# A two-layer graph network on one core: paired angles, a sum moved between passes, and indirect DMAs alternating one by one

## The chip, the cores and the metric

The kernel runs on one core of a Trainium2 chip. The metric is the time of one execution on the device, in microseconds (us). TensorE is called PE, its weight load PEld, VectorE DVE, ScalarE ACT, GpSimd POOL, and SyncE SP (SPq for its queue). SP does nothing but issue plain DMAs; POOL issues the indirect ones, which gather or scatter 128 rows by a list of indices.

## The reference, cut to what matters

There are 100,000 nodes with 160 features (64 scalars and 32 vectors of 3) and 25,000 edges, sorted by destination. Each layer norms the rows, takes relu, sends a message along each edge, sums the messages by destination, and adds the result to x.

```
h = relu(layernorm(x))
# layer 0
sc    = linear(h, sc_w)                      # every node
msg   = f(linear(h[src], lin1_w), edge_attr, silu(edge_scalars @ fc_w1) @ fc_w2)
mid   = segment_sum(msg, dst) / 4
conv  = linear(mid, lin2_w)
angle = 0.1 * (mid_s @ lin3_w) / sqrt(96) * node_attr
x1 = x + cos(angle) * sc * node_attr + sin(angle) * conv * node_attr
# layer 1
h1  = relu(layernorm(x1))
m   = g(h1[src], edge_attr; W1..W5)
agg = segment_sum(m, dst)
out = x1 + h1 + relu(linear(agg, Ws, Wv))
```

## The kernel before, in words

The work is done in three passes over DRAM. **Pass one** takes all nodes as if none had a message (dense part: x1, h1 and out = x1 + h1) and beside it computes the messages of layer 0 for 196 tiles of 128 edges (T = 196), sums them by destination, and stores the sums (`sum_tab`) and the own rows of the destinations (`own_tab`). It ends at about 1205 us. **Pass two** mends the nodes that have messages: for each of 49 groups (Q = 49) of four tiles it loads own rows and sums, makes x1 and h1, scatters h1 into `h1_all` and stores x1 + h1 in `y_tab`. **Pass three** gathers h1 of the sources, computes the messages of layer 1, sums them, adds y, and scatters the result into `out`.

The order of the work is written out by hand, engine by engine; semaphores tie the engines. Each engine's instructions run in the order in which they stand, so a wait holds up all that is behind it on its engine. `At(i, c)` is the number of a step in a loop; `q.times(m, plus)` is q*m + plus, `q.over(k, m, plus)` is (q // k)*m + plus, and `q.mod(k)` picks a buffer.

Pass two runs in steps. In step q **DVE** does (`p2_step`, L1647): the moments of group q, the first part of the scales of q-1 (L1592; it waits for the sines of q-1), the centring of q (L1553, L1554), the angles of q in eight short instructions (`p2_angle`, L1564 to L1581) strewn between the others, the sum x1 + h1 of group q-3 (`p2_y`, L1645), the rest of the scales of q-1, the self part of q-1 (L1610), the second norm of q-2 (L1636, L1235), x1 of q-1 (L1620) and its moments. **PE** transposes the centred rows of q and multiplies them; **ACT** does in step q (L938): the roots, the copies of q's transposed rows (L918, L919), h1 of q-2 (L911), the sines of q (L924). Sine and root need different tables, each loaded by an ACT_TABLE_LOAD. **SP** (L545) loads in its step v the own rows of v when x1(v-4) is done, then the sums of v-1, and then stores y(v-6). DVE's step q makes x1(q-1), so that SP's step v falls into DVE's step v-3. **POOL** scatters h1 of each group, four DMAs (L727).

Pass three has one slot per tile. In slot n DVE takes the vector products of tile n (`p3_features`, L1719), the outer part of message n-2 (L1739, which waits for PE), the dot and cross products of n (L1730 to L1732), the output of tile n-4 (`p3_out`, L1755: the instruction called yo below), the message sum of n-2 (L1745), and once in four slots the selectors (L1406). PE transposes the features of n-1, sums n-4 and multiplies n-2. ACT scales and copies. POOL (L746 to L774) issues two scatters of `out` (tiles n-4 and n-3), then two gathers of h1 rows (tiles n+6 and n+7), and so on. The four gathers of a group count up one semaphore, `m_g[j]`; DVE and ACT wait for all four (64) at the first tile of the group. The first instruction behind DVE's wait is a copy of indices (L1409). `y_tab` is loaded once a group into x1 (`p3_y`, L576).

Of the kernel before, what the change touches and what calls it, by code (L numbers as in the profile page):

```python
# [73 lines left out]
def gnn_kernel(nc, xa, src, dst, dst_rows, number, edges_in, scalars_in, scalars_t_in, wpack, out):  # L74
# [19 lines left out]
    y_tab = scratch("y_tab", (Q, P, GQ * D))  # L94
# [24 lines left out]
    with ExitStack() as ctx:  # L119
# [96 lines left out]
        trig = [two(f"trig{n}", [P, 2 * GQ]) for n in range(8)]  # L216
# [112 lines left out]
        r_y = sem("p2_y_ready")  # L329
        r_put = sem2("p2_h1_scattered")  # L330
        r_sty = sem2("p2_y_stored")
# [6 lines left out]
        m_y = sem2("p3_y_loaded")  # L338
        m_g = sem2("p3_h1_rows")
# [36 lines left out]
        def _(sp):  # L376
# [181 lines left out]
            for v in range(Q - 1, Q + 6):  # L558
                p2_step(At(0, v))
# [32 lines left out]
            for j in range(2):  # L592
                sp.wait_ge(r_sty[j], 16 * ((Q + 1 - j) // 2))
                sp.wait_ge(r_put[j], 64 * ((Q + 1 - j) // 2))
# [11 lines left out]
        def _(pool):  # L606
# [136 lines left out]
            pool.wait_ge(r_y, Q)  # L743


            def p3_gather(n):  # L746
# [3 lines left out]
                wait(pool, m_ft, n.times(1, -6))  # L750
                wait(pool, m_ss, n.times(1, -6))
                gather(h1_all, h1[j], D, i_src[j], m_g[j], (t, t + 1))

            def p3_scatter(n):
# [3 lines left out]
                pool.wait_ge(m_o, n.times(1, 2))  # L758
                scatter(out, yo[j], i_put[j], m_put[j], (t, t + 1))

            for n in range(0, 6, 2):
                p3_gather(At(0, n, 8))
            for n in range(0, 8, 2):
                if n >= 4:
                    p3_scatter(At(0, n - 4, 8))
                p3_gather(At(0, n + 6, 8))
            with pool.Fori(1, (Q - 3) // 2) as i:
                for c in range(0, 8, 2):
                    p3_scatter(At(i, c, 8) - 4)
                    p3_gather(At(i, c, 8) + 6)  # L770
            for n in range(T - 3 * GQ, T + 4, 2):
                p3_scatter(At(0, n - 4, 8))
                if n + 6 < T:
                    p3_gather(At(0, n + 6, 8))  # L774
# [3 lines left out]
        def _(act):  # L778
# [142 lines left out]
            def p2_sines(q):  # L921
                j = q.mod(2)
                act.wait_ge(r_ang, q.times(8, 8))
# [14 lines left out]
            def p2_step(q):  # L938
# [7 lines left out]
                if q.within(Q):  # L946
# [278 lines left out]
        def _(v):  # L1225
# [331 lines left out]
            def p2_angle(q, part):  # L1557

                j = q.mod(2)
                ang, turns, rest, arg = (trig[n][j] for n in range(4))  # L1560
                k = turns[:, GQ:2 * GQ]
                if part == 0:
                    v.wait_ge(r_cv[q.mod(4)], q.over(4, 16, 16))
                    ins = V.tensor_tensor(ang[:, 0:GQ], x3(cv[q.mod(4)], CW, GQ)[:, :, 0], x3(x_q[q.mod(4)], XW, GQ)[:, :, D],  # L1564
                                          ALU.mult)
                else:
                    v.wait_ge(r_ang, q.times(8, part))
                if part == 1:
                    ins = V.tensor_scalar(turns[:, 0:GQ], ang[:, 0:GQ], 1.0 / PI2, ROUND, ALU.mult, ALU.add)
                elif part == 2:  # L1570
                    ins = V.tensor_scalar(turns[:, GQ:2 * GQ], turns[:, 0:GQ], -ROUND, None, ALU.add)
                elif part == 3:
                    ins = V.scalar_tensor_tensor(rest[:, 0:GQ], k, -CA, ang[:, 0:GQ], ALU.mult, ALU.add)
                elif part == 4:
                    ins = V.scalar_tensor_tensor(rest[:, GQ:2 * GQ], k, -CB, rest[:, 0:GQ], ALU.mult, ALU.add)
                elif part == 5:
                    ins = V.scalar_tensor_tensor(ang[:, GQ:2 * GQ], k, -CC, rest[:, GQ:2 * GQ], ALU.mult, ALU.add)
                elif part == 6:
                    ins = V.tensor_scalar(arg[:, 0:GQ], ang[:, GQ:2 * GQ], PI_IN, -PI_IN, ALU.min, ALU.max)
                elif part == 7:  # L1580
                    ins = V.tensor_scalar(arg[:, GQ:2 * GQ], arg[:, 0:GQ], 0.5, None, ALU.mult)  # L1581
# [287 lines left out]
```

## Time and profile before

| | us |
|---|---|
| three runs | 2253.13, 2264.83, 2266.06 |
| their median | 2264.83 |
| the profiled execution, its time | 2256.09 |
| its span | 2254.3 |
| PE busy | 1753.3 (78%) |
| DVE busy | 1726.3 (77%) |
| POOL busy | 1517.9 (67%) |
| ACT busy | 1441.7 (64%) |

The span is the time from the first to the last instruction that the profiler saw. The busy shares are means over three passes of different kinds; what holds for one pass has to be read in a window of that pass. All durations below come from the one profiled execution. A busy time counts an instruction from its start to its end, and instructions of one engine overlap a little, so that the distance of two starts says more than a duration.

### The profile page before, as it was taken

What the parts mean: (1) busy time and instruction counts of PE and PEld (TensorE: products, weight loads), DVE (VectorE), ACT (ScalarE), POOL (GpSimd) and SP (SyncE); (2) the same over time, 40 slices, a digit from 0 to 9 for tenths busy, and PEclk for the clock granted to TensorE, in tenths of its full rate; (3) what the DMA queues carried; (4) which work ended last, traced back from release to release, by engine and by line L of the source; (5) the groups of instructions that cost most, each with busy time, mean ns of one, the idle gap of its engine ahead of it and who ended that gap; (6) DMA issues with size and microseconds to landing.
All of it is one profiled execution on the core that took longest, in us unless ns stands there. A gap on an engine that the chain in (4) does not pass through costs nothing.

```text
span 2254.3 us, 52147 instructions
## 1 busy us (share of the span) xinstructions
PE 1753.3 (78%) x12130; PEld 1645.3 (73%) x12130; DVE 1726.3 (77%) x6714; ACT 1441.7 (64%) x4193; POOL 1517.9 (67%) x1636
## 2 busy tenths in 40 slices
PE   6898988898998989898995666666467767677665
PEld 2798988888888989888885665565366666666665
DVE  2699899989999998999896999999455555555553
ACT  2588887788787878877886777777333333333332
POOL 3378888888878788878873555555566666666664
PEclk9999999999999999999996556666599999989998
DMA  5477677767777777767775445554333333333331
GB/s 188 144 245 248 246 247 243 246 245 250 248 254 247 250 250 244 245 243 245 244 243 189 151 157 170 168 161 162 93 88 86 96 94 96 97 90 95 100 94 58
DMA packets 176960, 408.91 MB, mean 181 GB/s; under 512 B 43774, under 2 KB 73788, under 8 KB 176766
## 3 DMA queue, kind: packets, MB, share of 16 engines
q1 hardware_dynamic: 129694, 333.90, 43.0%
q0 software_dynamic: 47232, 74.64, 11.8%
q8 instruction: 11, 0.18, 0.0%
q14 instruction: 23, 0.19, 0.0%
HBM read 199.20 MB, written 216.96 MB: 185 GB/s over the span
## 4 chain that ended last, share of the span: by engine, by line
PE 35%; DVE 25%; issue 15%; ACT 10%; DMA 8%; POOL 4%; DVEq 1%; SPq 1%; ACTq 0%; POOLq 0%
DVE st L1231 6%; DMA h<-h_all,i_src 5%; PE bank L1007 5%; ACT h L786 3%; PE bank L1002 3%; DVE st_e L1231 3%; PE bank L1008 3%; PE bank L1111 3%; PE bank L1183 2%; PE bank L1085 2%; DMA h_all<-h,i_put 2%; PE bank L1056 2%; DVE part L1610 2%; POOL h L622 2%; DVE x L1379 2%
## 5 line engine op out<-in xcount | busy, mean ns | idle before, releaser
L678 POOL TENSOR_TENSOR yo<-x,h 128x320 f32<-128x320 f32 x392 | 363.1, 947 | 122.6 <-ACT h L786 115.3
L1007 PE MATMUL bank<-wp,hT 128*128 128x160 f32 x1568 | 374.2, 320 | 0.0
L786 ACT ACTIVATE h<-x,nmr,inv 128x160 f32<-128x160 f32 x784 | 342.0, 514 | 0.6 <-DVE nmr L1235 0.6
L629 POOL DMA_INDIRECT h_all<-h,i_put x196 | 206.1, 1051 | 190.5 <-issue 163.2
L629 POOL DMA_INDIRECT out<-yo,i_put x196 | 200.1, 1021 | 187.7 <-DVE yo L1755 119.5
L1007 PE MATMUL bank<-wp,eT 128*128 128x160 f32 x784 | 262.6, 428 | 49.4 <-ACT eR L919 43.6
L1008 PE MATMUL bank<-wp,hR 128*128 128x64 f32 x1568 | 259.4, 247 | 0.0
L1183 PE MATMUL bank<-ident,feat 128*128 128x128 f32 x392 | 90.4, 314 | 213.7 <-DVE feat L1732 187.7
L1008 PEld LDWEIGHTS bank<-wp,hR 128*128 128x128 f32 x1568 | 255.5, 190 | 0.0
L1379 DVE SCALAR_TENSOR_TENSOR x<-bank,scl,x_all 128x160 f32<-128x160 f32 x784 | 253.8, 365 | 1.0 <-PE bank L1008 0.6
L622 POOL DMA_INDIRECT x_e<-in_xa,i_src x200 | 211.5, 1057 | 44.5 <-issue 18.0
L622 POOL DMA_INDIRECT h<-h_all,i_src x196 | 196.9, 1005 | 62.8 <-issue 57.3
L1007 PEld LDWEIGHTS bank<-wp,hT 128*128 128x128 f32 x1568 | 237.8, 192 | 0.0
L622 POOL DMA_INDIRECT x_d<-in_xa,i_dst x196 | 197.2, 1006 | 59.0 <-issue 58.3
L1739 DVE TENSOR_TENSOR xr<-bank,q_ed 128x96 f32<-128x96 f32 x196 | 50.3, 256 | 237.0 <-PE bank L1193 237.0
L1183 PEld LDWEIGHTS bank<-ident,feat 128*128 128x128 f32 x392 | 41.1, 146 | 246.9 <-DVE feat L1732 156.8
L1231 DVE BATCH_NORM_STATS2 st<-x 128x6 f32<-128x320 f32 x490 | 218.3, 486 | 0.0
L971 ACT ACTIVATE tot<-bank 128x160 f32<-128x160 f32 x196 | 59.0, 301 | 248.5 <-PE bank L1205 247.7
L1007 PEld LDWEIGHTS bank<-wp,eT 128*128 128x128 f32 x784 | 163.0, 258 | 65.7 <-issue 34.9
L965 ACT ACTIVATE feat<-h,q_ed 128x160 f32<-128x160 f32 x196 | 83.5, 426 | 162.7 <-DMA h<-h_all,i_src 157.9
L1111 PE MATMUL bank<-ident,feat 128*128 128x128 f32 x588 | 101.4, 282 | 109.0 <-DVE feat L1453 61.8
L1008 PEld LDWEIGHTS bank<-wp,eR 128*128 128x128 f32 x784 | 180.4, 261 | 0.0
(164 smaller groups left out, 5556.7 us busy)
## 6 DMA issues: line engine op xcount, KB each, us to landing
x_all<-in_xa SPq DMA_DIRECT2D x98, 644.0 KB, 5.7
h_all<-h SPq DMA_DIRECT2D x98, 640.0 KB, 3.7
out<-yo SPq DMA_DIRECT2D x98, 640.0 KB, 4.0
q_row<-row_tab SPq DMA_DIRECT2D x98, 256.0 KB, 3.6
sum_tab<-tot SPq DMA_DIRECT2D x49, 322.0 KB, 3.7
own_tab<-x_d SPq DMA_DIRECT2D x49, 322.0 KB
x_all<-own_tab SPq DMA_DIRECT2D x49, 322.0 KB, 2.9
y_tab<-yo SPq DMA_DIRECT2D x49, 320.0 KB
```

The lines of the kernel that those rows point to most:

```text
L622: nc.gpsimd.indirect_dma_start(into[:, t * width:(t + 1) * width], None, rows, bass.IndirectOffsetOnAxis(ap=index[:, t:t + 1], axis=0)).th ...
L629: nc.gpsimd.indirect_dma_start(rows, bass.IndirectOffsetOnAxis(ap=index[:, t:t + 1], axis=0), tiles_of[:, t * D:(t + 1) * D], None, bounds ...
L678: ins = nc.gpsimd.tensor_tensor(yo[j][:, a:b], x1[j][:, a:b], h1[j][:, a:b], ALU.add)
L786: ins = nc.scalar.activation(h1[j][:, k * D:(k + 1) * D], x1[j][:, k * D:(k + 1) * D], ACT.Relu, bias=nmr2[j][:, k:k + 1], scale=inv2[j][: ...
L965: nc.scalar.activation(f[:, 0:D], h, ACT.Copy, scale=ed(j, t, 0, 1))
L1002: nc.tensor.transpose(ps_main[:, t * P:(t + 1) * P], main[:, t * P:(t + 1) * P], ident[:, :])
L1007: nc.tensor.matmul(dst_ps, main[:, t * P:(t + 1) * P], wp[:, w:w + D], start=True, stop=False)
L1008: return nc.tensor.matmul(dst_ps[:, 0:DS], rest[:, :], wp[:, w + D + t * DS:w + D + (t + 1) * DS], start=False, stop=True)
L1111: ins = nc.tensor.transpose(bank[4][:, c * P:(c + 1) * P], f[:, at:at + P], ident[:, :])
L1183: nc.tensor.transpose(b[:, c * P:(c + 1) * P], f[:, c * P:(c + 1) * P], ident[:, :])
L1231: return V.bn_stats(st[:, 2 * pair:2 * pair + 2, :].rearrange("p g k -> p (g k)"), two_rows[:, 0:D, :])
L1379: ins = V.scalar_tensor_tensor(x1[j][:, k * D:(k + 1) * D], bank[2 + pair % 2][:, k % 2 * D:(k % 2 + 1) * D], scl1[u.mod(4)][:, k:k + 1], ...
```

## The change

It has three parts. **Angles.** `p2_angle` runs in even steps alone and takes groups q and q+1 together; its first part waits for own rows and sums of both. The sines and the halved sine's square are taken once for two groups as well. **The sum** x1 + h1 leaves pass two: SP stores x1 and h1 of each group in two tables, pass three loads both, and DVE adds them there once per four tiles (`p3_x1_h1`). On SP the store now stands first in a step, for group v-5. **Pass three's DMAs:** POOL alternates one scatter (tile n-4) and one gather (tile n+5); each tile's gather has a semaphore of its own, and DVE and ACT wait for it tile by tile. The copy of the gather's indices moves from the first to the last tile of a group.

```diff
             def p2_store(q):
-                sp.wait_ge(r_y, q.times(1, 1))
-                sp.dma_start(y_tab[q.times(1)], yo[q.mod(2)][:, 0:GQ * D]).then_inc(r_sty[q.mod(2)], 16)
+                j = q.mod(2)
+                sp.wait_ge(r_x1, q.times(2, 2))
+                sp.dma_start(x1_tab[q.times(1)], x1[j][:, 0:GQ * D]).then_inc(r_stx[j], 16)
+                sp.wait_ge(r_h1, q.times(1, 1))
+                sp.dma_start(h1_tab[q.times(1)], h1[j][:, 0:GQ * D]).then_inc(r_sth[j], 16)
 
 
             def p2_step(v):
+                if (v - 5).within(Q):
+                    p2_store(v - 5)
                 if v.within(Q):
                     p2_own(v)
                 if (v - 1).within(Q):
                     p2_sums(v - 1)
-                if (v - 6).within(Q):
-                    p2_store(v - 6)
 
             for v in range(8):
                 p2_step(At(0, v))
             with sp.Fori(2, Q // 4) as i:
                 for c in range(4):
                     p2_step(At(i, c))
-            for v in range(Q - 1, Q + 6):
+            for v in range(Q - 1, Q + 5):
                 p2_step(At(0, v))
...
             def p3_y(q):
                 j = q.mod(2)
                 wait(sp, m_o, q.times(GQ, -GQ))
-                sp.dma_start(x1[j][:, 0:GQ * D], y_tab[q.times(1)]).then_inc(m_y[j], 16)
+                sp.dma_start(x1[j][:, 0:GQ * D], x1_tab[q.times(1)]).then_inc(m_y[j], 16)
+                sp.dma_start(hb[j][:, 0:GQ * D], h1_tab[q.times(1)]).then_inc(m_y[j], 16)
 
...
             p2_scatter(At(0, Q - 1))
             for j in range(2):
                 pool.wait_ge(r_put[j], 64 * ((Q + 1 - j) // 2))
-            pool.wait_ge(r_y, Q)
+                pool.wait_ge(r_sth[j], 16 * ((Q + 1 - j) // 2))
 
 
             def p3_gather(n):
                 j, t = n.c // GQ % 2, n.mod(4)
                 if t == 0:
                     pool.wait_ge(m_ix, n.over(4, 1, 1))
-                wait(pool, m_ft, n.times(1, -6))
-                wait(pool, m_ss, n.times(1, -6))
-                gather(h1_all, h1[j], D, i_src[j], m_g[j], (t, t + 1))
+                wait(pool, m_ft, n.times(1, -7))
+                wait(pool, m_ss, n.times(1, -7))
+                gather(h1_all, h1[j], D, i_src[j], m_g[n.mod(8)], (t,))
 
             def p3_scatter(n):
                 j, t = n.c // GQ % 2, n.mod(4)
                 if t == 0:
                     pool.wait_ge(m_px, n.over(4, 1, 1))
-                pool.wait_ge(m_o, n.times(1, 2))
-                scatter(out, yo[j], i_put[j], m_put[j], (t, t + 1))
-
-            for n in range(0, 6, 2):
+                pool.wait_ge(m_o, n.times(1, 1))
+                scatter(out, yo[j], i_put[j], m_put[j], (t,))
+
+            for n in range(5):
                 p3_gather(At(0, n, 8))
-            for n in range(0, 8, 2):
-                if n >= 4:
-                    p3_scatter(At(0, n - 4, 8))
-                p3_gather(At(0, n + 6, 8))
+            for n in range(8):
+                if n >= GQ:
+                    p3_scatter(At(0, n - GQ, 8))
+                p3_gather(At(0, n + 5, 8))
...
             def p2_h1(q):
                 j = q.mod(2)
                 act.wait_ge(r_nmr, q.times(2, 2))
-                wait(act, r_y, q.times(1, -1))
+                wait(act, r_sth[j], q.over(2, 16))
                 wait(act, r_put[j], q.over(2, 64))
...
             def p2_sines(q):
-                j = q.mod(2)
-                act.wait_ge(r_ang, q.times(8, 8))
+                j = q.mod(4) // 2
+                act.wait_ge(r_ang, q.over(2, 8, 8))
                 nc.scalar.activation(trig[4][j][:, :], trig[3][j][:, :], ACT.Sin).then_inc(r_sin, 1)
...
             def p3_scalars(n):
                 j, t = n.c // GQ % 2, n.mod(4)
                 if t == 0:
-                    act.wait_ge(m_g[j], n.over(8, 64, 64))
                     act.wait_ge(m_tb[j], n.over(8, 16, 16))
+                act.wait_ge(m_g[n.mod(8)], n.over(8, 16, 16))
...
             def p2_angle(q, part):
 
-                j = q.mod(2)
-                ang, turns, rest, arg = (trig[n][j] for n in range(4))
-                k = turns[:, GQ:2 * GQ]
+                ang, turns, rest, arg = (trig[n][q.mod(4) // 2] for n in range(4))
+                k = turns[:, GP:2 * GP]
                 if part == 0:
-                    v.wait_ge(r_cv[q.mod(4)], q.over(4, 16, 16))
-                    ins = V.tensor_tensor(ang[:, 0:GQ], x3(cv[q.mod(4)], CW, GQ)[:, :, 0], x3(x_q[q.mod(4)], XW, GQ)[:, :, D],
-                                          ALU.mult)
+                    for d in range(2):
+                        if (q + d).within(Q):
+                            m = (q + d).mod(4)
+                            v.wait_ge(r_g[m], (q + d).over(4, 16, 16))
+                            v.wait_ge(r_cv[m], (q + d).over(4, 16, 16))
+                            ins = V.tensor_tensor(ang[:, d * GQ:(d + 1) * GQ], x3(cv[m], CW, GQ)[:, :, 0],
...
 
                 j = q.mod(2)
-                sines, half2, scales = trig[4][j], trig[5][j], trig[6][j]
+                sines, half2, scales = (trig[n][q.mod(4) // 2] for n in (4, 5, 6))
+                a, b = j * GQ, (j + 1) * GQ
                 attr = x3(x_q[q.mod(4)], XW, GQ)[:, :, D]
                 if part == 0:
                     v.wait_ge(r_sq1, q.times(1, 1))
-                    v.wait_ge(r_sin, q.times(1, 1))
+                    v.wait_ge(r_sin, q.over(2, 1, 1))
                     V.reciprocal(inv_e[j][:, :], sd_e[j][:, :])
-                    V.tensor_tensor(scales[:, GQ:2 * GQ], sines[:, 0:GQ], attr, ALU.mult)
-                    ins = V.tensor_tensor(half2[:, 0:GQ], sines[:, GQ:2 * GQ], sines[:, GQ:2 * GQ], ALU.mult)
+                    ins = V.tensor_tensor(scales[:, GP + a:GP + b], sines[:, a:b], attr, ALU.mult)
+                    if j == 0:
+                        ins = V.tensor_tensor(half2[:, 0:GP], sines[:, GP:2 * GP], sines[:, GP:2 * GP], ALU.mult)
                 elif part == 1:
                     v.wait_ge(r_scl, q.times(4, 1))
-                    V.tensor_tensor(scl_e[j][:, :], inv_e[j][:, :], attr, ALU.mult)
-                    ins = V.tensor_scalar(half2[:, GQ:2 * GQ], half2[:, 0:GQ], -2.0, 1.0, ALU.mult, ALU.add)
+                    ins = V.tensor_tensor(scl_e[j][:, :], inv_e[j][:, :], attr, ALU.mult)
+                    if j == 0:
+                        ins = V.tensor_scalar(half2[:, GP:2 * GP], half2[:, 0:GP], -2.0, 1.0, ALU.mult, ALU.add)
                 else:
                     v.wait_ge(r_scl, q.times(4, 2))
...
             def p2_x1(q):
                 j = q.mod(2)
                 v.wait_ge(r_scl, q.times(4, 4))
-                wait(v, r_y, q.times(1, -1))
+                wait(v, r_h1, q.times(1, -1))
+                wait(v, r_stx[j], q.over(2, 16))
                 for t in range(GQ):
...
-            def p2_y(q):
-                j = q.mod(2)
-                v.wait_ge(r_h1, q.times(1, 1))
-                wait(v, r_sty[j], q.over(2, 16))
-                V.tensor_tensor(yo[j][:, 0:GQ * D], x1[j][:, 0:GQ * D], h1[j][:, 0:GQ * D], ALU.add).then_inc(r_y, 1)
-
...
                 if a:
                     p2_centre(q)
+                if e:
                     p2_angle(q, 0)
-                if (q - 3).within(Q):
-                    p2_y(q - 3)
-                if a:
+                if e:
                     p2_angle(q, 1)
                 if b:
                     p2_scales(q - 1, 1)
-                if a:
+                if e:
                     p2_angle(q, 2)
                 if b:
                     p2_scales(q - 1, 2)
-                if a:
+                if e:
                     p2_angle(q, 3)
                 if b:
                     p2_self(q - 1)
-                if a:
...
             def p3_features(n):
                 j, t = n.c // 4 % 2, n.mod(4)
                 if t == 0:
-                    v.wait_ge(m_g[j], n.over(8, 64, 64))
                     v.wait_ge(m_tb[j], n.over(8, 16, 16))
-                    if (n + 8).within(T):
-                        index_copy(i_src[j], t_src, At(n.i, n.c // GQ, 2) + 2, m_ix)
+                v.wait_ge(m_g[n.mod(8)], n.over(8, 16, 16))
+                if t == GQ - 1 and (n + 5).within(T):
...
+            def p3_x1_h1(n):
+                j = n.c // GQ % 2
+                v.wait_ge(m_y[j], n.over(8, 32, 32))
+                V.tensor_tensor(x1[j][:, 0:GQ * D], x1[j][:, 0:GQ * D], hb[j][:, 0:GQ * D], ALU.add).then_inc(m_ys, 1)
+
             def p3_out(n):
                 j, t = n.c // GQ % 2, n.mod(4)
                 if t == 0:
-                    v.wait_ge(m_y[j], n.over(8, 16, 16))
+                    v.wait_ge(m_ys, n.over(4, 1, 1))
                     wait(v, m_put[j], n.over(8, 64))
                     index_copy(i_put[j], t_put, At(n.i, n.c // GQ, 2), m_px)
...
                     p3_message_sum(n - 2)
+                if n.mod(4) == 2 and (n - 2).within(T):
+                    p3_x1_h1(n - 2)
```

The rest of the diff carries the same names through (semaphores, tables, the columns of `trig`, the loops' ends) and makes the other parts of `p2_angle` twice as wide.

## Rows read from the trace of the kernel before

**Rows 1.** Windows of passes two, three: busy us per engine, PEclk, DMA share, GB/s.

```profile
1195.00:1590.00 395.00, 249.77 (x1036) 225.02 (x1034) 356.51 (x1573) 287.55 (x550) 205.86 (x198) 0.60 0.50 163
...
1613.00:2242.00 629.00, 441.06 (x2925) 405.10 (x2924) 331.36 (x1505) 233.11 (x967) 384.62 (x380) 0.93 0.32 90
```

**Rows 2.** Pass two's timeline, DVE, ACT, SP: start us, us, instruction, [idle before, releaser].

```profile
1492.04 0.18 DVE L1592 RECIPROCAL inv_e<-sd_e 128x4 f32<-128x4 f32 x1 [0.40 <-ACT trig L924]
...
1493.17 0.82 DVE L1645 TENSOR_TENSOR yo<-x,h 128x640 f32<-128x640 f32 x1
1493.91 0.16 DVE L1569 TENSOR_SCALAR trig<-trig 128x4 f32<-128x4 f32 x1
...
1496.01 0.16 DVE L1235 SCALAR_TENSOR_TENSOR nmr<-st,inv 128x4 f32<-128x4 f32 x1
1496.22 1.27 DVE L1620 SCALAR_TENSOR_TENSOR x<-cv,trig,part 128x160 f32<-128x160 f32 x4
...
1499.82 0.18 DVE L1592 RECIPROCAL inv_e<-sd_e 128x4 f32<-128x4 f32 x1 [0.46 <-ACT trig L924]
...
1522.78 0.18 DVE L1592 RECIPROCAL inv_e<-sd_e 128x4 f32<-128x4 f32 x1 [0.40 <-ACT trig L924]
...
1495.10 0.27 ACT L919 ACTIVATE eR<-bank 128x128 f32<-128x128 f32 x1
1496.34 1.76 ACT L911 ACTIVATE h<-x,nmr,inv 128x160 f32<-128x160 f32 x4 [0.97 <-DVE nmr L1235]
...
1497.66 0.34 SPq L534 DMA_DIRECT2D x_all<-own_tab  x1
1498.31 0.33 SPq L538 DMA_DIRECT2D hb<-sum_tab  x1
```

**Rows 3.** DMA issues of pass two: size, median us from issue to landing.

```profile
x_all<-own_tab SPq DMA_DIRECT2D x21, 322.0 KB, 2.9
...
cv<-sum_tab SPq DMA_DIRECT2D x11, 322.0 KB, 3.8
```

**Rows 4.** Timeline of pass two's start, SP and DVE: the first sums.

```profile
1209.59 0.43 SPq L538 DMA_DIRECT2D cv<-sum_tab  x1
...
1215.30 0.17 DVE L1564 TENSOR_TENSOR trig<-cv,x_all 128x4 f32<-128x4 f32 x1 [1.86 <-DMA cv<-sum_tab]
```

**Rows 5.** Timeline of pass three over one group's border, DVE, then POOL.

```profile
1907.61 0.31 DVE L1755 SCALAR_TENSOR_TENSOR yo<-tot,x 128x160 f32<-128x160 f32 x1
...
1909.85 0.26 DVE L1739 TENSOR_TENSOR xr<-bank,q_ed 128x96 f32<-128x96 f32 x1 [1.32 <-PE bank L1193]
...
1912.69 0.26 DVE L1739 TENSOR_TENSOR xr<-bank,q_ed 128x96 f32<-128x96 f32 x1 [1.32 <-PE bank L1193]
...
1916.17 0.17 DVE L1409 COPY i_src<-t_src 128x4 int32 x1 [1.75 <-DMA h<-h_all,i_src]
...
1916.61 0.25 DVE L1739 TENSOR_TENSOR xr<-bank,q_ed 128x96 f32<-128x96 f32 x1
...
1907.32 0.98 POOL L622 DMA_INDIRECT h<-h_all,i_src  x1 [0.30 <-issue]
1908.85 1.02 POOL L629 DMA_INDIRECT out<-yo,i_put  x1 [0.55 <-issue]
...
1911.47 0.99 POOL L622 DMA_INDIRECT h<-h_all,i_src  x1 [0.30 <-issue]
1912.76 0.98 POOL L622 DMA_INDIRECT h<-h_all,i_src  x1 [0.30 <-issue]
```

**Rows 6.** Waits of pass three, 1613 to 2242 us: us in total, times, longest.

```profile
POOL out L629 <- DVE yo L1755: 117.6, 47, 13.3
DVE i_src L1409 <- DMA h<-h_all,i_src: 60.5, 38, 2.3
```

**Rows 7.** Windows in pass three, columns as in rows 1.

```profile
1888.00:1892.00 4.00, 2.04 (x18) 1.88 (x16) 2.10 (x10) 1.65 (x7) 3.08 (x4) 0.99 0.58 186
1892.00:1900.00 8.00, 6.49 (x30) 6.00 (x29) 2.94 (x14) 2.39 (x10) 4.04 (x5) 0.58 0.16 40
```

More of the change, by code:

```diff
@@ L93, in gnn_kernel @@
     hid_tab = scratch("hid_tab", (Q, P, 2 * P))
-    y_tab = scratch("y_tab", (Q, P, GQ * D))
+    x1_tab = scratch("x1_tab", (Q, P, GQ * D))
+    h1_tab = scratch("h1_tab", (Q, P, GQ * D))
     h1_all = scratch("h1_all", (N, D))
@@ L215, in gnn_kernel @@
         cv = [c[:, :] for c in two("cv", [P, GQ * CW])] + [hb[i][:, 0:GQ * CW] for i in range(2)]
-        trig = [two(f"trig{n}", [P, 2 * GQ]) for n in range(8)]
+        trig = [two(f"trig{n}", [P, 4 * GQ]) for n in range(7)]
+        GP = 2 * GQ
         st_e = two("st_e", [P, GQ, 3])
@@ L328, in gnn_kernel @@
         r_h1 = sem("p2_h1_ready")
-        r_y = sem("p2_y_ready")
         r_put = sem2("p2_h1_scattered")
-        r_sty = sem2("p2_y_stored")
+        r_stx = sem2("p2_x1_stored")
+        r_sth = sem2("p2_h1_stored")
         m_ix = sem("p3_index_copied")
@@ L337, in gnn_kernel @@
         m_ca = sem2("p3_carry_loaded")
-        m_y = sem2("p3_y_loaded")
-        m_g = sem2("p3_h1_rows")
+        m_y = sem2("p3_x1_and_h1_loaded")
+        m_ys = sem("p3_x1_and_h1_added")
+        m_g = [sem(f"p3_h1_rows{i}") for i in range(2 * GQ)]
         m_sc = sem("p3_selectors_ready")
@@ L757, in p3_scatter @@
                     pool.wait_ge(m_px, n.over(4, 1, 1))
-                pool.wait_ge(m_o, n.times(1, 2))
-                scatter(out, yo[j], i_put[j], m_put[j], (t, t + 1))
-            for n in range(0, 6, 2):
+                pool.wait_ge(m_o, n.times(1, 1))
+                scatter(out, yo[j], i_put[j], m_put[j], (t,))
+            for n in range(5):
                 p3_gather(At(0, n, 8))
-            for n in range(0, 8, 2):
-                if n >= 4:
-                    p3_scatter(At(0, n - 4, 8))
-                p3_gather(At(0, n + 6, 8))
+            for n in range(8):
+                if n >= GQ:
+                    p3_scatter(At(0, n - GQ, 8))
+                p3_gather(At(0, n + 5, 8))
             with pool.Fori(1, (Q - 3) // 2) as i:
[L768 to L774, printed above, removed]
+                for c in range(8):
+                    p3_scatter(At(i, c, 8) - GQ)
+                    p3_gather(At(i, c, 8) + 5)
+            for n in range(T - 3 * GQ, T + GQ):
+                p3_scatter(At(0, n - GQ, 8))
+                if n + 5 < T:
+                    p3_gather(At(0, n + 5, 8))
         @block.scalar
@@ L945, in p2_step @@
                     p2_h1(q - 2)
-                if q.within(Q):
+                if q.within(Q) and q.mod(2) == 0:
                     p2_sines(q)
@@ L1566, in p2_angle @@
                 else:
-                    v.wait_ge(r_ang, q.times(8, part))
+                    v.wait_ge(r_ang, q.over(2, 8, part))
                 if part == 1:
-                    ins = V.tensor_scalar(turns[:, 0:GQ], ang[:, 0:GQ], 1.0 / PI2, ROUND, ALU.mult, ALU.add)
+                    ins = V.tensor_scalar(turns[:, 0:GP], ang[:, 0:GP], 1.0 / PI2, ROUND, ALU.mult, ALU.add)
                 elif part == 2:
-                    ins = V.tensor_scalar(turns[:, GQ:2 * GQ], turns[:, 0:GQ], -ROUND, None, ALU.add)
+                    ins = V.tensor_scalar(turns[:, GP:2 * GP], turns[:, 0:GP], -ROUND, None, ALU.add)
@@ L1639, in p2_norm2 @@
                     shift_of(nmr2[j], st2[j], inv2[j], GQ, r_nmr)
-            def p2_y(q):
-                j = q.mod(2)
-                v.wait_ge(r_h1, q.times(1, 1))
-                wait(v, r_sty[j], q.over(2, 16))
-                V.tensor_tensor(yo[j][:, 0:GQ * D], x1[j][:, 0:GQ * D], h1[j][:, 0:GQ * D], ALU.add).then_inc(r_y, 1)
             def p2_step(q):
                 a, b, c = q.within(Q), (q - 1).within(Q), (q - 2).within(Q)
+                e = a and q.mod(2) == 0
                 if a:
@@ L1683, in p2_step @@
                     p2_x1(q - 1)
-                if a:
+                if e:
                     p2_angle(q, 6)
@@ L1700, in _ @@
                     p2_step(At(i, c))
-            for q in range(Q - 1, Q + 3):
+            for q in range(Q - 1, Q + 2):
                 p2_step(At(0, q))
@@ L1782, in _ @@
             for n in range(16):
-                if n == GQ:
-                    for j in range(2):
-                        v.wait_ge(r_sty[j], 16 * ((Q + 1 - j) // 2))
                 p3_slot(At(0, n, 8))
```

27 lines of the change are left out of this document (16 added, 11 removed).

## The prediction

> **What bounds the kernel now.** I read the stages first [rows 1], then one period of each changed stage in order of time, then what each wait is for. Pass two (49 groups) is a DVE stage: DVE is busy 356.51 of 395 us, while PE, at 249.77, runs at a mean granted clock of 0.60, most of the time at the lower level. Pass three (196 tiles) takes 629 us, 3.21 a tile, and no engine in it is busy for more than 441.06; its clock is 0.93. So it is bound by a chain or by waits.
>
> Pass two is a loop over two engines. Four steps take 1522.78 - 1492.04 = 30.74 us, so two take 15.37 [rows 2]. In one: `p2_scales` starts at 1492.04 (L1592), the shift of the second norm (L1235) at 1496.01 and is over at 1496.17; ACT makes h1 from 1496.34 to 1498.10, loads the sine table and takes the sines; only then does DVE go on, at 1499.82, after 0.46 idle. The reader is to see that DVE has no other idle time, and that ACT's part of the loop ends last by this little.
>
> Pass three runs at PE and DVE's own pace between gathers: L1739 at 1909.85 and 1912.69, 2.84 apart. The next comes 3.92 later, at 1916.61, since DVE stood for 1.75 until the fourth gather of the group, issued at 1912.76, had landed [rows 5]. There are 38 such waits, 60.5 us together [rows 6].
>
> **The change, part by part.** *Sum out of pass two.* `p2_y` is 0.82 us of DVE in each step and starts 0.74 before the next instruction (1493.17 to 1493.91, rows 2). Taken alone that would be worth 0.74 x 49 = 36 us.
>
> *Angles once per two groups.* The 16 instructions of two groups become 9. They are short, 0.07 to 0.2 apart, and several stand in gaps that waits leave anyway. ACT saves one pair of table loads and one sine in two steps, and the 0.46 idle goes in every second step. Without a new wait I get 6.2 us for an odd step and about 7.1 for an even one, 13.3 against 15.37.
>
> *The new wait.* The first angle instruction of even q now needs the sums of q+1 as well. SP loads them in its step q+2. That step now begins with the store of group q-3, which waits for h1(q-3), made by ACT in step q-1; the loads of own rows (q+2) and then of the sums (q+1) are behind it on SP. Before, the sums of q came off SP one step earlier, and only x1 held them up. So the work queued behind this wait is all of DVE's even step, and through it h1 and the sines. I work out the loop from landing to landing:
> - From landing to `p2_scales` of the odd step: 0.3 for the wait's end and the second product, then what stood from L1569 to L1592, 1499.82 - 1493.91 = 5.91. Together 6.2. ACT's h1 and sine are in it.
> - Odd step to the end of h1: DVE without sum and angles would reach L1235's end in 3.1, so the copies of the transposed rows end later (L919, 1495.10 + 0.27 - 1492.04 = 3.33); h1 adds 0.03 + 1.76. Together 5.1.
> - h1's end to landing: SP needs 0.17 (x1 ends 1497.49, its load goes at 1497.66, rows 2), then the h1 store, own rows, sums, some 0.5 apart (1497.66 and 1498.31 are two such issues): the sums are issued 1.2 after h1's end. As second transfer such a load lands 3.8 after issue [rows 3]: 4.9 in all. As third in a burst, at 1209.59, it held DVE until 1215.30, 5.7 [rows 4]: 6.9 in all. The change makes it third, but that burst had more behind it; I take 5.8.
>
> The sum is 6.2 + 5.1 + 5.8 = 17.1 for two groups against 15.37, which is 1.73 x 24 = **42 us more**; the ends are 16.2 and 18.2, 20 and 68 us more. The saving of the two edits above is not seen: DVE is idle for it. The other new waits cost nothing: x1's and h1's stores are issued one to two steps before their buffers are written again, against some 3 us of landing.
>
> *Traffic.* Pass two stores 320 KB more a group at a DMA share of 0.50, pass three loads 320 KB more per four tiles at 0.32 [rows 1]. It costs nothing beyond the landing above; the two loads of pass three start right after the last output of the group two back and have two and a half slots (7 us) to land, where one takes about 3 [rows 3]. SP's later loads there move by 0.5, with slots to spare.
>
> *The sum in pass three*, 0.82 per four tiles, stands at the end of a slot in which DVE waits 1.32 for PE before L1739 [rows 5]. It is covered by that; if the cover went, it would cost 0.82 x 49 = 40 us.
>
> *Gathers and scatters singly.* Now the pair for tiles 2 and 3 of a group is issued behind two scatters: yo ends at 1907.92, the scatter starts at 1908.85, the gathers at 1911.47 and 1912.76, landing about 1915.9, where DVE wants it at 1914.4. After, the gather of tile n+5 goes after one scatter: 0.93 + 1.3 + 3.2 = 5.4 us after yo of slot n, and it is wanted five slots later, some 11 after yo. The stall goes with 5.9 to spare. POOL's two operations of a tile take 1.02 + 0.30 + 0.98 + 0.30 = 2.6, below the slot of 2.83 [rows 5]. Next to be late is the chain PE-DVE itself, 196 x 2.83 = 555 us against 629, 74 less. Some 38 x 1.08 = 41 of it are the stalls. The other 33 is the clock: mean 0.93 of two levels means 88 us at the lower one. One such fall follows a stretch in which PE was busy only 2.04 of 4 us, at a stall [rows 7]. I expect falls to go mostly with the stalls and leave 6 us: **68 us less**, ends 41 (all falls stay) and 74.
>
> *Head and tail.* Tile 0 no longer waits for three more gathers, 3 x 1.29 = 3.9, of which I take 3; the last scatter leaves one operation sooner, 1.3. About 4 less.
>
> **A page against the rows.** The sum above takes a third transfer's landing from rows. The Trainium skill, "DMA: Bandwidth & Descriptors", section "Anatomy of one DMA", gives a DMA a fixed cost of about 2.0 us plus its bytes at 436 GB/s; by it a third transfer would be complete 2.0 + 0.964 MB/436 GB/s = 4.2 us after the first is issued. It is a fit for DMAs of another queue than SP's. For a lone transfer it gives 2.7, and the trace has 2.9 [rows 3]; for a third the trace has far more. By the page the sum would be 8 us more in pass two in place of 42.
>
> **Sum.** The profiled execution took 2256.09 (span 2254.3). 2256.1 + 42 - 68 - 4 = **2226**, 1.3% less. The median of the runs shown is 2264.83, 8.7 above that execution, and the runs lie from 2253.13 to 2266.06; I don't shift the number. About 1%, 23 us, is what a measurement of this kernel can tell from no change.
>
> **Rivals.**
> - *A, queued transfers pass almost freely.* A store, own rows and sums stream at the full rate and the sums land 4.4 after h1's end: 15.7 for two groups, 8 us more. With 68 to 74 less in pass three: 2190. For it: the second transfer lands only 0.9 later after issue than the first. Against: rows 4. The page above gives this time.
> - *B, the clock falls without stalls too.* PE is idle a quarter of each slot anyway. Pass three then gives 41 only: 2256 + 42 - 41 - 4 = 2253. For it: most of the 38 stalls have no fall behind them. Against: rows 7.
> - *C, slower.* POOL's start-up after yo doesn't overlap with the gather ahead of it. Each tile's pair is then a closed loop of 0.93 + 1.02 + 0.30 + 0.98 = 3.2 us, in place of one start-up per two tiles; pass three stays at 196 x 3.2 = 629, and the time is 2256 + 42 - 4 = 2294. It decides from a mean slot of 3.13 on: above that the time is over 2279, slower by 1%. For it: 47 of the 98 pairs of scatters waited for yo [rows 6]. Against: the scatter at 1908.85 came only 0.55 after the gather before it had ended (1907.32 + 0.98, rows 5), so most of the 0.93 ran beside the gather.
> - *D, the wait on the sums isn't there*, because I misread SP's order: pass two gives 2.07 x 24 = 50 less, and the time is 2256 - 50 - 72 = 2134. Little speaks for it.
>
> **Chances.** My case 0.60, A 0.11, B 0.16, C 0.09, D 0.04. My case with its bounds (landing 4.9 to 6.9, pass three 41 to 74) spans 2198 to 2270 at its ends, two thirds of it below 2233. Faster by over 1%: 0.40 + 0.11 + 0.04 and a little of B, 0.55. Within 1%: 0.19 of mine and 0.14 of B, 0.33. Slower: C and a corner of mine, 0.12. The range takes in A, B and nearly all of my case, 2186 to 2264; C, D and the corners are left out.
>
> **What would show it.** In pass two after: two steps of about 17.1 us, DVE idle some 4 us once in two steps ahead of the second angle product, put down to the transfer of the sums; no sine wait in even steps. If two steps are near 13.3, D holds; near 15.7, A. In pass three: L1739 every 2.83 us through group borders, no wait for gathers, POOL idle about 0.2 a tile, and the granted clock above 0.97. A clock still near 0.93 is B; slots of 3.2 with POOL late are C. I am wrong if the time is outside 2186 to 2264, and wrong in the reason if pass two gets shorter.

## The result, and the profile after

The changed kernel takes 2206.64 us (median of 4 runs, 2205.67 to 2208.61) where the kernel before took 2263.95 (median of 4, 2253.13 to 2266.06): a ratio of 0.9757, interval 0.9725 to 0.9789. 2226 was forecast, with 2186 to 2264 as range. The span of the profiled execution is 2203.9, 50.4 less than before. The parts of the table are read from the two profiled executions; the start ahead of pass two is 1.1 longer.

| | before | after | forecast |
|---|---|---|---|
| pass two, first to last start of `p2_scales` (48 steps) | 366.3 | 383.3 (+17) | +42 |
| pass three, first to last start of the outer part (195 slots) | 627.6 | 560.3 (-67) | -68 |
| between the two | 29.8 | 28.1 (-1.6) | -3 |
| after the last | 13.0 | 13.5 (+0.4) | -1 |

The windows of the two passes (columns as in rows 1, which they answer; pass two 415 us here):

```profile
1195.00:1610.00 415.00, 224.21 (x1033) 202.44 (x1033) 310.66 (x1313) 222.60 (x482) 199.55 (x200) 0.66 0.60 195
1640.00:2190.00 550.00, 397.91 (x2881) 364.20 (x2881) 363.40 (x1529) 230.31 (x957) 388.29 (x379) 1.00 0.44 130
```

DVE's busy share in pass two fell from 356.51 of 395 to 310.66 of 415: less work in more time. In pass three the granted clock is 1.00, the upper of its two levels, where its mean was 0.93.

Pass two, timeline of DVE, then ACT, then SP (answers to rows 2; L1604 is L1592 of before, L1575 L1564, L1243 L1235):

```profile
1485.90 0.17 DVE L1575 TENSOR_TENSOR trig<-hb,x_all 128x4 f32<-128x4 f32 x1 [3.48 <-DMA hb<-sum_tab]
...
1491.72 0.18 DVE L1604 RECIPROCAL inv_e<-sd_e 128x4 f32<-128x4 f32 x1 [0.31 <-ACT trig L932]
...
1497.75 0.17 DVE L1604 RECIPROCAL inv_e<-sd_e 128x4 f32<-128x4 f32 x1
...
1498.69 0.15 DVE L1575 TENSOR_TENSOR trig<-cv,x_all 128x4 f32<-128x4 f32 x1
1501.79 0.17 DVE L1575 TENSOR_TENSOR trig<-cv,x_all 128x4 f32<-128x4 f32 x1 [2.94 <-DMA cv<-sum_tab]
...
1494.75 0.27 ACT L927 ACTIVATE eR<-bank 128x128 f32<-128x128 f32 x1
1494.91 1.75 ACT L919 ACTIVATE h<-x,nmr,inv 128x160 f32<-128x160 f32 x4
...
1496.68 0.35 SPq L548 DMA_DIRECT2D h_tab<-h  x1
1497.28 0.35 SPq L537 DMA_DIRECT2D x_all<-own_tab  x1
1497.73 0.40 SPq L541 DMA_DIRECT2D cv<-sum_tab  x1
```

DVE's period of two steps is 1501.79 - 1485.90 = 15.89. The long wait in it is 2.94 before the second angle product (3.48 a period earlier), put down to the transfer of the sums; the sines still cost 0.31 once in two steps. The load was issued at 1497.73, after h1 had ended at 1496.66 and after h1's store and the own rows had gone out. The odd step (1491.72 to 1497.75) takes 6.03, the even one about 10.2. This period is one of the shorter ones: the median of all is 16.2 (before: 15.3). DVE's waits for the sums in the whole pass (1218 to 1600 us: us in total, times, longest) come to 68.7:

```profile
DVE trig L1575 <- DMA hb<-sum_tab: 35.2, 12, 3.5
DVE trig L1575 <- DMA cv<-sum_tab: 33.5, 11, 3.6
```

The DMA issues of pass two, 1400 to 1580 us (answers to rows 3):

```profile
x_all<-own_tab SPq DMA_DIRECT2D x23, 322.0 KB, 3.0
...
h_tab<-h SPq DMA_DIRECT2D x22, 320.0 KB, 2.2
hb<-sum_tab SPq DMA_DIRECT2D x12, 322.0 KB, 4.2
cv<-sum_tab SPq DMA_DIRECT2D x11, 322.0 KB, 4.0
```

Pass three over a group's border, DVE, then POOL (answers to rows 5; L1749 is L1739 of before):

```profile
1907.84 0.26 DVE L1749 TENSOR_TENSOR xr<-bank,q_ed 128x96 f32<-128x96 f32 x1 [1.32 <-PE bank L1201]
...
1908.92 0.81 DVE L1761 TENSOR_TENSOR x<-x,hb 128x640 f32<-128x640 f32 x1
...
1910.68 0.26 DVE L1749 TENSOR_TENSOR xr<-bank,q_ed 128x96 f32<-128x96 f32 x1 [0.51 <-PE bank L1201]
...
1913.52 0.26 DVE L1749 TENSOR_TENSOR xr<-bank,q_ed 128x96 f32<-128x96 f32 x1 [0.72 <-PE bank L1201]
...
1909.68 1.01 POOL L637 DMA_INDIRECT out<-yo,i_put  x1 [0.55 <-issue]
1911.00 0.97 POOL L630 DMA_INDIRECT h<-h_all,i_src  x1 [0.30 <-issue]
1912.53 1.17 POOL L637 DMA_INDIRECT out<-yo,i_put  x1 [0.55 <-issue]
```

The outer part comes every 2.84 us across the border, and POOL has 0.30 to 0.55 left between its operations. Among the waits from 1640 to 2190 us there is none for a gather any more; only at the pass's start two tiles wait for theirs. DVE's and PE's largest, and POOL's for the output:

```profile
DVE xr L1749 <- PE bank L1201: 185.5, 192, 1.7
PE bank L1191 <- DVE feat L1742: 152.1, 191, 0.9
...
POOL out L637 <- DVE yo L1770: 19.7, 9, 6.3
```

### The profile page after: what moved, and what is told of

The parts are those of the page before. It is cut to its first block, busy times and chain, and to the rows that moved or that the text cites. A ratio compares the mean times of both kernels' runs of the same rounds, so it can differ in the third digit from the quotient of the medians.

```text
span 2203.9 us, 52353 instructions
## 1 busy us (share of the span) xinstructions
PE 1692.9 (77%) x12130; PEld 1589.0 (72%) x12130; DVE 1717.1 (78%) x6498; ACT 1374.2 (62%) x4121; POOL 1511.6 (69%) x1636
## 4 chain that ended last, share of the span: by engine, by line
PE 44%; DVE 24%; issue 11%; ACT 9%; DMA 6%; SPq 2%; POOL 2%; DVEq 1%; ACTq 0%; POOLq 0%
DVE st L1239 6%; PE bank L1015 5%; PE bank L1010 4%; PE bank L1191 4%; PE bank L1199 3%; ACT h L794 3%; PE bank L1016 3%; PE bank L1119 3%; PE bank L1212 3%; DVE st_e L1239 3%; PE bank L1200 2%; PE bank L1213 2%; DMA cv<-sum_tab 2%; DMA hb<-sum_tab 2%; PE bank L1093 2%
## 5 line engine op out<-in xcount | busy, mean ns | idle before, releaser
L637 POOL DMA_INDIRECT h_all<-h,i_put x196 | 197.6, 1008 | 216.2 <-issue 187.0
L637 POOL DMA_INDIRECT out<-yo,i_put x196 | 205.3, 1048 | 109.2 <-issue 88.3
L1015 PE MATMUL bank<-wp,eT 128*128 128x160 f32 x784 | 241.3, 397 | 49.4 <-ACT eR L927 43.7
L1749 DVE TENSOR_TENSOR xr<-bank,q_ed 128x96 f32<-128x96 f32 x196 | 50.4, 257 | 192.7 <-PE bank L1201 192.7
L1015 PEld LDWEIGHTS bank<-wp,eT 128*128 128x128 f32 x784 | 149.2, 237 | 67.5 <-issue 35.0
L1010 PE MATMUL bank<-ident,h_e 128*128 128x128 f32 x392 | 81.4, 345 | 137.1 <-DVE hr_e L1562 136.6
L1239 DVE BATCH_NORM_STATS2 st<-x_all 128x6 f32<-128x320 f32 x392 | 166.1, 485 | 0.0
```

What stands on the lines that cost most here:

```text
L637: nc.gpsimd.indirect_dma_start(rows, bass.IndirectOffsetOnAxis(ap=index[:, t:t + 1], axis=0), tiles_of[:, t * D:(t + 1) * D], None, bounds ...
L1010: nc.tensor.transpose(ps_main[:, t * P:(t + 1) * P], main[:, t * P:(t + 1) * P], ident[:, :])
L1015: nc.tensor.matmul(dst_ps, main[:, t * P:(t + 1) * P], wp[:, w:w + D], start=True, stop=False)
L1239: return V.bn_stats(st[:, 2 * pair:2 * pair + 2, :].rearrange("p g k -> p (g k)"), two_rows[:, 0:D, :])
```

## The experiments

Each ratio is against the kernel before, timed on the same chip; its interval stands behind it. The chips differ by run, so times in us from different runs agree less closely than a few us. A diff shows the lines that matter; `...` stands for what is left out. The length of pass two or three in a run is that from the first to the last start of the same instructions as in the table above, in its profiled execution.

**e1, sums early.** The wait that the change brought, taken away by an earlier load.

```diff
-                if (v - 1).within(Q):
-                    p2_sums(v - 1)
+                if v.within(Q):
+                    p2_sums(v)
```

> The changed kernel with one edit: SP loads the sums of group v in the same step as the own rows of v, one step earlier than before. Theory (the wait on the second group's sums costs pass two about 3 us in every two steps): the wait goes, two steps take 13.3 us in place of 16.2, 24 x 2.9 = 70 us less than the changed kernel, so about 2137 us. Rival (pass two is held by its traffic of 1.6 MB a group, and the wait only shows where it is held): the wait turns up at another load, two steps stay above 15.5, and the time is above 2188.

Measured 2138.98, ratio 0.943 (0.9364 to 0.9496). The two angle products now follow each other:

```profile
1408.08 0.29 DVE L1562 TENSOR_TENSOR hr_e<-x_all,st_e 128x128 f32<-128x128 f32 x1
...
1408.28 0.28 DVE L1575 TENSOR_TENSOR trig<-hb,x_all 128x4 f32<-128x4 f32 x2
1408.59 0.17 DVE L1580 TENSOR_SCALAR trig<-trig 128x8 f32<-128x8 f32 x1
```

The two instructions of L1575 stand together with no idle time before them. Odd steps take 6.0, even ones 6.9 to 7.3, 13.1 together in the mean. Pass two takes 313.6 in place of 383.3, 69.7 less, which is what DVE had waited for the sums (68.7). The traffic was not the bound: the same bytes move in less time (DMA share of the pass 0.72 in place of 0.60). This is also the best kernel of the study.

**e2, stores last.** SP's `p2_store(v - 5)` moved behind the loads of its step.

```diff
-                if (v - 5).within(Q):
-                    p2_store(v - 5)
                 if v.within(Q):
                     p2_own(v)
                 if (v - 1).within(Q):
                     p2_sums(v - 1)
+                if (v - 5).within(Q):
+                    p2_store(v - 5)
```

> The changed kernel with SP's two stores put behind the loads of a step, as the store of y stood. Theory (the loads are late because the wait for h1 and h1's store stand before them on SP): the sums of q+1 are issued 0.8 after x1's end and land 3.8 later as second transfer, 1.3 us sooner in two steps; 24 x 1.3 = 31 less than the changed kernel, 2175 us. Rival (traffic): no difference, 2206.

Measured 2180.38, 0.9606 (0.954 to 0.9672); two steps take about 15.0. Pass two takes 356.8, 26.5 less than in the changed kernel. So some 26 us of the wait's price is the store of h1 and the wait for h1 ahead of the loads; the other 43 go only when the sums are loaded one step earlier (e1).

**e3, angles unpaired.** `p2_angle`, `p2_scales` and the sines as before, in every step; all else as changed.

```diff
...
-                e = a and q.mod(2) == 0
+                e = a
```

> The changed kernel with the angles of each group taken in its own step, as before; stores, the moved sum and pass three stay as changed. Theory: the wait on sums comes from the pairing alone. Without it a step takes 7.68 less 0.8 for the sum that left, two take 13.8 in place of 16.2, 24 x 2.4 = 58 less: 2148 us. Rival (the stores of x1 and h1 hold pass two): two steps stay at 16, 2206 us or more, since the instructions of the angles come back.

Measured 2166.73, 0.9544 (0.9478 to 0.961). The stores hold nothing, and the pairing as made costs about 2 in 100 (0.9757 against 0.9544). But two steps take 14.4 and not 13.8. Timeline of DVE in this kernel:

```profile
1405.02 0.16 DVE L1571 TENSOR_TENSOR trig<-hb,x_all 128x4 f32<-128x4 f32 x1
...
1405.21 0.17 DVE L1576 TENSOR_SCALAR trig<-trig 128x4 f32<-128x4 f32 x1
...
1405.46 0.29 DVE L1578 TENSOR_SCALAR trig<-trig 128x4 f32<-128x4 f32 x1
...
1405.89 0.16 DVE L1580 SCALAR_TENSOR_TENSOR trig<-trig 128x4 f32<-128x4 f32 x1
1406.07 1.26 DVE L1617 SCALAR_TENSOR_TENSOR part<-bank,trig,x_all 128x160 f32<-128x160 f32 x4
```

From the angle product to the self part (L1617) it is 1.05 us; in the kernel before, with the sum in the stretch, it is 1.44 (the two lines below). So the sum's going shortens this stretch by 0.40 and the whole step by 0.45 ((366.3 - 344.7) / 48), not by 0.74:

```profile
1493.10 0.16 DVE L1564 TENSOR_TENSOR trig<-cv,x_all 128x4 f32<-128x4 f32 x1
...
1494.54 1.26 DVE L1610 SCALAR_TENSOR_TENSOR part<-bank,trig,x_all 128x160 f32<-128x160 f32 x4
```

By the code each part of the angle waits for the one before, and the sum filled some of that time. That this is the reason is argued and not tested; two of the small instructions also take longer here (0.36 and 0.29) than in rows 2.

**e7, unpaired and early.** Both edits.

```diff
...
-                e = a and q.mod(2) == 0
+                e = a
...
-                    p2_sums(v - 1)
+                    p2_sums(v)
```

> The changed kernel with unpaired angles and the sums loaded one step earlier. Against the run with early sums and paired angles it gives the worth of the pairing without any wait. Theory: 0.5 us in two steps, 12 us in all: this one about 2148, the paired one 2137; and it is the same as unpaired angles with late sums, since an unpaired step doesn't wait. Rival: the pairing is worth the full 0.9 us of its eight instructions less in two steps and the sines' wait, 1.5 us and more: 35 us.

Measured 2168.62, 0.955 (0.9494 to 0.9606), the same as e3, as both theories have it. Against e1 the pairing is worth 30 us (pass two takes 345.1 and 313.6), so here the rival's 35 was nearer than my 12: in every second step the angle's instructions go, and one of the two waits for sines with them.

**e9, early sums and stores last.**

```diff
-                if (v - 5).within(Q):
-                    p2_store(v - 5)
                 if v.within(Q):
                     p2_own(v)
-                if (v - 1).within(Q):
-                    p2_sums(v - 1)
+                if v.within(Q):
+                    p2_sums(v)
+                if (v - 5).within(Q):
+                    p2_store(v - 5)
```

> The changed kernel with the sums loaded one step earlier and the stores behind the loads. Theory (with the sums early nothing waits for SP in pass two): the same as with early sums alone, 0.943 of the kernel before, 2139 us. Rival (the loads of own rows are next to be late): up to 10 us less.

Measured 2141.81, 0.9432 (0.939 to 0.9474), the same as e1 within the intervals. The theory holds for the time but not to the letter: no load is waited for, but with the stores behind the loads DVE's x1 now waits for the store of the x1 before it, 5.2 us in all, and pass two takes 317.7 in place of 313.6 (waits between 1218 and 1535 us):

```profile
DVE x L1636 <- DMA x_tab<-x: 5.2, 17, 0.5
```

**e5, pass three's DMAs alone.** The kernel before with the changed `p3_gather`, `p3_scatter` and a signal for each tile.

```diff
...
-                gather(h1_all, h1[j], D, i_src[j], m_g[j], (t, t + 1))
+                gather(h1_all, h1[j], D, i_src[j], m_g[n.mod(8)], (t,))
...
```

> The kernel before with pass three's DMAs as changed (one scatter, one gather, a signal for each tile), passes one and two as before. Theory: pass three alone gives all of the gain and more, 67 us less than before: 0.970 of it, some 2195 us. Rival (the gain of pass three leans on the moved sum): less than 40 us.

Measured 2191.64, 0.9656 (0.9599 to 0.9713). Pass three takes 564.1 in place of 627.6, at a clock of 1.00 between 1625 and 2175 us. This third of the change is worth more than the whole.

**e4, pass three's DMAs as before** in the changed kernel: pairs of scatters and gathers, and one signal for a group's four gathers.

```diff
...
-                gather(h1_all, h1[j], D, i_src[j], m_g[n.mod(8)], (t,))
+                gather(h1_all, h1[j], D, i_src[j], m_g[j], (t, t + 1))
...
```

> The changed kernel with pass three's indirect DMAs as before: pairs, six tiles ahead, one signal for a group's four. Theory: the stalls at group borders come back, and with them the falls of the clock; pass three is back at 3.21 a tile and a clock of 0.93, 67 us more: 2273 us. Rival (the falls went for another reason than the stalls): the stalls cost 38 x 1.08 = 41 us and the clock stays near 1.0: 2247 us.

Measured 2322.86, 1.0241 (1.0165 to 1.0317): the stalls and the falls come back, and with 50 us more than I expected; pass three takes 668.9. **e11 and e12** ask for those. Both stand on top of e4's edit. e11 leaves out pass three's load of h1, and with it all but 4 columns of the sum:

```diff
-                sp.dma_start(hb[j][:, 0:GQ * D], h1_tab[q.times(1)]).then_inc(m_y[j], 16)
...
```

> Pass three's DMAs as before in the changed kernel (the run at 2323 us), with the load of h1 and all but 4 columns of the sum left out, so that the output lacks h1. It asks why that run was 117 us slower than the changed kernel and not 67. Theory (the second load of 320 KB, issued beside the group's last gather, lands that gather some 0.3 us later, and longer stalls bring more falls of the clock): without it the stalls are as in the kernel before and the time is near 2273. Rival (the sum on DVE does it, through the order of its engine or by lengthening a gather's issue, 1.13 against 0.98 us): no better than the run in which the sum alone is cut.

e12 keeps the load and cuts the sum to 4 columns:

```diff
...
-                V.tensor_tensor(x1[j][:, 0:GQ * D], x1[j][:, 0:GQ * D], hb[j][:, 0:GQ * D], ALU.add).then_inc(m_ys, 1)
+                V.tensor_tensor(x1[j][:, 0:4], x1[j][:, 0:4], hb[j][:, 0:4], ALU.add).then_inc(m_ys, 1)
```

> The same with all but 4 columns of the sum left out (the output lacks h1) and both loads kept. Theory (the load): within 10 us of 2323. Rival (the sum on DVE): 2290 or less, most of the way to 2273.

Measured: e11 2277.17, 1.0054 (1.0015 to 1.0093); e12 2291.64, 1.0118 (1.0072 to 1.0164). Pass three takes 625.7 in e11, as in the kernel before, and 638.8 in e12. The waits for gathers and the window 1700 to 2200 of e4:

```profile
DVE i_src L1417 <- DMA h<-h_all,i_src: 67.4, 32, 3.2
...
1700.00:2200.00 500.00, 341.65 (x2182) 314.54 (x2182) 276.39 (x1166) 173.92 (x728) 300.40 (x292) 0.91 0.38 111
```

The same of e12, and of e11 (L1416):

```profile
DVE i_src L1417 <- DMA h<-h_all,i_src: 49.7, 29, 2.0
...
1700.00:2200.00 500.00, 351.61 (x2294) 323.32 (x2294) 265.12 (x1224) 183.46 (x765) 312.07 (x308) 0.91 0.39 117
```

```profile
DVE i_src L1416 <- DMA h<-h_all,i_src: 54.0, 32, 2.0
...
1700.00:2200.00 500.00, 347.18 (x2340) 318.58 (x2338) 270.48 (x1248) 186.86 (x780) 315.03 (x312) 0.94 0.33 94
```

Of the 46 us between e4 and e11 the sum on DVE gives some 31, and it shows in the stall (67.4 us for 32 waits against 49.7 for 29). The other 15, between e12 and e11, aren't clear of noise: the intervals of the two ratios overlap, and e11's ten times lie between 2270.58 and 2302.54, e12's four between 2284.75 and 2297.04. In the traces the stalls of the two are alike and the clock is 0.94 in e11 and 0.91 in e12, but that is one execution of each. So the sum is shown as a cause; whether the load is one stays open, and so does how the sum lengthens the stall.

**e6, one signal, single order.** The changed order of POOL, but DVE and ACT wait for all four gathers at a group's first tile.

```diff
...
-                gather(h1_all, h1[j], D, i_src[j], m_g[n.mod(8)], (t,))
+                gather(h1_all, h1[j], D, i_src[j], m_g[j], (t,))
...
```

> The changed kernel with pass three's order of single gathers and scatters kept, but one signal for the four gathers of a group: DVE and ACT wait for all four at its first tile. Theory (what ends the stall is that the group's last gather stands behind one scatter and not behind two and a gather): that gather lands 5.4 us after the output of its slot and is wanted 6.1 after, so the time stays within 5 us of the changed kernel, 2207. Rival (the signal for each tile is what ends it): stalls of 1 us or more at each border and falls of the clock, 20 to 67 us more.

Measured 2346.19, 1.0333 (1.0271 to 1.0395). DVE and POOL at one border:

```profile
1905.15 0.31 DVE L1770 SCALAR_TENSOR_TENSOR yo<-tot,x 128x160 f32<-128x160 f32 x1
...
1908.46 0.68 DVE L1414 TENSOR_TENSOR same<-q_row,f_dst 128x512 f32<-128x512 int32 x1
1911.61 0.46 DVE L1729 TENSOR_TENSOR prod<-h,q_ed 128x288 f32<-128x288 f32 x1 [2.48 <-DMA h<-h_all,i_src]
...
1906.38 1.01 POOL L637 DMA_INDIRECT out<-yo,i_put  x1 [0.55 <-issue]
1907.70 0.98 POOL L630 DMA_INDIRECT h<-h_all,i_src  x1 [0.30 <-issue]
```

My theory fell. I had counted 2 us too many: from the output at 1905.15 to where the first features of the next group could start it is not 6.1 us but 4 (1909.1, by the 0.6 from the selectors to the features in the changed kernel), and the gather issued at 1907.70, the group's last, released them at 1911.61. With a shared signal, alternating singly is no better than pairs and by the traces worse: pass three takes 702.7 us against 668.9 in e4, and the times of e6 (2342.78 to 2348.94) lie above those of e4 (2316.43 to 2329.19), though the intervals of the ratios overlap.

**e8, pairs, a signal for each tile.** The order of before, six tiles ahead, with the changed signals.

```diff
...
                 gather(h1_all, h1[j], D, i_src[j], m_g[n.mod(8)], (t,))
+                gather(h1_all, h1[j], D, i_src[j], m_g[n.mod(8) + 1], (t + 1,))
...
```

> The changed kernel with pass three's DMAs in pairs, six tiles ahead, as before, but with a signal of its own for each tile's gather. Theory (what counts is that a tile waits for its own gather alone): no tile waits, since each is gathered four slots or more ahead; L1739's counterpart comes every 2.83 us, the clock is 1.0, and the time is that of the changed kernel, 2207, within 6. Rival (single alternation is needed too): POOL's four operations in a row make a later gather of the pair late; stalls and falls of the clock, 2230 or more.

Measured 2209.18, 0.9722 (0.968 to 0.9763); the change has 0.9757 (0.9725 to 0.9789), and the intervals overlap. Between 1640 and 2190 us DVE waits for no gather. Four kernels differ only in pass three's DMAs (pairs run six tiles ahead, single ones five). Their pass three takes, in us:

| | one signal per group | one signal per tile |
|---|---|---|
| pairs | 668.9 (e4) | 562.8 (e8) |
| one by one | 702.7 (e6) | 560.3 (the change) |

So it is the signal and not the order of the DMAs that gives the gain.

**e10, the sum of pass three cut** to 4 columns, with the edit of e12, in the changed kernel.

> The changed kernel with pass three's sum of x1 and h1 cut to the first 4 of 640 columns, so that its output lacks h1; loads and signals stay. Theory (the sum is covered by DVE's wait for PE): the time stays at 2207, within 4. Rival (it is on the path): 49 x 0.7 = 34 us less.

Measured 2209.54, 0.9724 (0.9682 to 0.9767); pass three takes 562.4 without the sum and 560.3 with it. The sum is covered, as long as no tile waits for its gather.

## Why the prediction was right

- *The number.* 2206.64 lies in the range, 19 below the 2226 forecast; the span fell by 50.4 where the parts forecast 30. It isn't as close in its parts: pass two grew by 25 less than forecast, and four small terms gave 5 back (1.1 ahead of pass two, 0.7 in pass three, 1.4 and 1.4 between and behind). The term for pass two, 17 for 42, lies below its own lower end of 20. Rival A had 8 there and 2190 in all, and was nearer than my case in both; two steps of 16.2 lie between its 15.7 and my 17.1. That the total lies in the range is in part luck: the range was wide enough for both.
- *Pass two pays a new wait.* Right in place and sign, by its trace, and e1, e2 and e3 show the price: 69.7 us by the traces of e1 and the change (0.9757 - 0.943 of the ratios makes it 74), where 24 x 3.8 (17.1 - 13.3) gave 91. All three terms were too large. In the period shown, 5.13 from h1's end to DVE's going on (1.07 to the issue and 4.06 to landing and start) for 5.8, 5.8 for 6.2, and 4.9 for 5.1. The row that I leaned toward for the landing, 5.7 as third in a burst, had four more loads behind it; third behind a store a load takes 4.0 to 4.2, near the second's 3.8 of [rows 3]. Whether the burst was slow for those four or for other traffic no run shows. The two ends of the pass, where a pair is shorter (14.1 and 12.7), make most of the difference between 16.2 a pair and the mean of 16.0.
- *Slips in the working.* My case's upper end is 2256 + 68 - 41 - 4 = 2279, not 2270. The two issues shown as "some 0.5 apart" are 0.65 apart; in the changed kernel they are 0.60 and 0.45. By the parts given, "faster by over 1%" adds up to about 0.57 and "slower" to 0.10. None of this moves the forecast.
- *What the two edits are worth without the wait.* 13.3 forecast, 13.1 in e1. Right in sum, wrong in parts: I put 0.74 a step on the sum leaving; e3 shows 0.45. That left 0.6 in two steps for the pairing; e7 against e1 shows 1.3.
- *The third transfer by the page.* The estimate by the Trainium skill's "DMA: Bandwidth & Descriptors", section "Anatomy of one DMA", is 4.2 us from the first issue; measured from h1's store (1496.68) to DVE at 1501.79, 5.1. The rows gave 5.6. The measurement lies between, somewhat nearer the rows.
- *Stalls and clock in pass three.* Right, 67 for 68, and e5 shows 63.5 by itself. That the falls would go with the stalls is right too: the clock is 1.00 without stalls and 0.89 to 0.94 with them (the kernel before, e4, e6, e11, e12). Rival B fell. The 6 us that I left for falls are something else: in the trace once in eight tiles a slot takes 3.05 and the next 2.91.
- *Why the stall goes.* The prediction gave two reasons in one sum: the gather goes behind one scatter and not two, and its tile is wanted some 11 us after the output of its slot. Only the second is the cause, and it is the signal for each tile that brings it. With a shared signal the group's last gather is wanted 4 us after the output that it follows (e6), with its own some 11. That the order helps was the wrong half. e8 shows the gain without the new order, e6 none with the new order alone. The number was right since both parts came together.
- *POOL's start-up overlaps with the operation before.* Right: 0.55 after the last operation's end, as in rows 5. Rival C fell.
- *The sum in pass three is covered.* Right (e10). If the cover goes it costs some 31 us (e4 against e12); I had 40.
- *Head and tail.* -1.6 and +0.4 for -3 and -1.

## What to carry to other kernels

When a step is paired to save instructions, ask what input of the second half is loaded last, and move that load in the same edit: here one line on SP turned a cost of 40 us (2206.64 against e3's 2166.73) into a gain of 30 (e1 against e7). A signal that counts up several transfers makes the first user wait for the last of them; here one signal for each user was worth the whole gain, and the reordering nothing. An instruction may fill time that its neighbours would spend waiting, and is then worth less than its own time when it goes.

## What was not expected of the hardware

- The end of short stalls gave more than their own length. In pass three before, a slot at a stall was some 1.1 us longer, 38 x 1.08 = 41 us; the whole pass became 67 shorter, and the granted clock rose from 0.93 to 1.00. By this estimate some 26 us are the clock's. The fall at 1892 us [rows 7] came after a stall in which PE had been idle for 1.96:

```profile
1890.97 0.43 PE L1183 MATMUL bank<-ident,feat 128*128 128x128 f32 x2 [1.96 <-DVE feat L1732]
```

- A 320 KB store ahead of a load delays it little: a load of the sums as third transfer lands 4.0 to 4.2 after its issue, as second 3.8 (medians).
- In e4 the sum of 128x640 on DVE (1839.48 to 1840.29) runs into one of POOL's issues; that gather, at 1840.03, took 1.13 us where others take 0.98. Whether the sum is the reason wasn't tested.
